# A softplus attention on one core: in each beat ScalarE takes the pending logarithm first and the exponentials second

## What is computed

```python
q, k, v = split(x @ w_qkv.T);  k_y = x @ w_ky.T          # 16 heads of 16
L   = einsum('bhqd,bhkd->bhqk', q, k) / 4
L_y = einsum('bhqd,bhkd->bhqk', q, k_y) / 4
agg = sum(exp(clip(L_y, -15, 15)) * causal, -1) + EPS
r   = log(abs(L) + EPS) - log(agg + EPS)
w   = softplus(r) * causal
A   = w / (sum(w, -1) + EPS)
x   = layernorm(x + (A @ v) @ w_proj.T)
x   = layernorm(x + ffn(x))                              # 256 -> 1024 -> 1024 -> 1024 -> 256
```

## Time and profile before

| | |
|---|---|
| device time, median of 3 runs | 1398.88 us (1397.62 to 1398.89) |
| the profiled execution: its own time | 1398.2 us |
| its span, first to last instruction | 1396.4 us |
| PE busy in the span | 1280.9 us (92%) |
| PE weight loads | 817.6 us (59%) |
| DVE busy | 718.2 us (51%) |
| ACT busy | 614.8 us (44%) |
| POOL busy | 113.3 us (8%) |
| mean granted TensorE clock | 0.972 |

### The profile page before, as it was taken

The page is one execution under the profiler, slowest core; times in us unless marked ns, Lnnn a source line. Parts: engine busy times, 40 slices in busy tenths (PEclk is TensorE's granted clock), DMA queues, the critical chain, the costliest instruction groups (busy, mean ns, idle before and its releaser), DMA issues.

```text
span 1396.4 us, 22945 instructions
## 1 busy us (share of the span) xinstructions
PE 1280.9 (92%) x8310; PEld 817.6 (59%) x8310; DVE 718.2 (51%) x1223; ACT 614.8 (44%) x810; POOL 113.3 (8%) x140
## 2 busy tenths in 40 slices
PE   5888999999898989977399999999999999999996
PEld 1433444434343434433278778787787878878785
DVE  2456777677676776566243532535326353353523
ACT  3566666666666666655042322323223241232411
POOL 1111121111111121110000000000000000000000
PEclk8999999999999999998589999999999999999998
DMA  2002222132122221000290000000000000000000
GB/s 74 16 16 69 92 75 77 60 102 78 60 90 90 90 71 57 1 31 31 70 331 15 16 15 15 30 15 19 11 15 30 15 30 0 15 30 15 30 0 16
DMA packets 31943, 66.89 MB, mean 48 GB/s; under 512 B 2848, under 2 KB 8608, under 8 KB 31904
## 3 DMA queue, kind: packets, MB, share of 16 engines
q1 hardware_dynamic: 31904, 66.35, 14.3%
HBM read 46.42 MB, written 19.92 MB: 48 GB/s over the span
## 4 chain that ended last, share of the span: by engine, by line
issue 50%; POOL 0%; DVE 0%; POOLq 0%; DVEq 0%
POOL f_rstd L809 0%; DVE f_res L816 0%; POOLq L909 0%; DVEq L821 0%; POOL f_minus_half L907 0%; POOLq L83 0%
## 5 line engine op out<-in xcount | busy, mean ns | idle before, releaser
L935 ACT ACTIVATE f_h_full<-f_layer_bank,f_scales 128x512 f32<-128x512 f32 x128 | 88.0, 687 | 354.8 <-PE f_layer_bank L1049 354.7
L500 DVE TENSOR_TENSOR w_ring<-score_banks,keep 128x1024 int32<-128x1024 int32 (+1 forms) x192 | 191.6, 1040 | 46.9 <-PE score_banks L649 46.9
L353 ACT ACTIVATE e_ring<-score_banks 128x1024 f32<-128x1024 f32 (+1 forms) x192 | 158.8, 879 | 122.8 <-PE score_banks L649 122.0
L1049 PE MATMUL f_layer_bank<-f_ha_hi,f_w_all 128*128 128x512 f32 x512 | 204.7, 400 | 2.7 <-DVE f_h_full L977 2.3
L1049 PE MATMUL f_layer_bank<-f_hb_hi,f_w_all 128*128 128x512 f32 x512 | 202.8, 396 | 0.0
L1049 PE MATMUL f_layer_bank<-f_ha_lo,f_w_all 128*128 128x512 f32 x512 | 202.1, 395 | 0.0
L1049 PE MATMUL f_layer_bank<-f_hb_lo,f_w_all 128*128 128x512 f32 x512 | 202.0, 395 | 0.0
L491 DVE TENSOR_SCALAR e_ring<-e_ring 128x2048 f32<-128x2048 f32 (+1 forms) x96 | 100.5, 1046 | 122.3 <-ACT e_ring L353 122.3
L360 ACT ACTIVATE w_ring<-w_ring 128x2048 f32<-128x2048 f32 (+1 forms) x96 | 156.8, 1633 | 8.6 <-DVE w_ring L500 8.3
L287 POOL TENSOR_SCALAR_AFFINE_SELECT e_ring<-e_ring 128x512 f32<-128x512 f32 (+1 forms) x96 | 78.5, 818 | 516.5 <-DVE e_ring L491 516.5
L675 PE MATMUL acc_bank<-w_ring,v_aug 128*32 128x512 f32 (+3 forms) x1024 | 91.2, 452 | 27.8 <-ACT w_ring L360 27.8
(11 more groups left out here) (101 smaller groups left out, 1535.0 us busy)
## 6 DMA issues: line engine op xcount, KB each, us to landing
piece<-in_wf SPq DMA_DIRECT2D x44, 256.0 KB, 2.9
wf_copy<-piece SPq DMA_DIRECT2D x44, 256.0 KB, 3.0
f_w_all<-wf_copy SPq DMA_DIRECT2D x2, 4096.0 KB, 26.4
f_x_turn<-x SPq DMA_DIRECT2D x9, 512.0 KB, 3.2
xq<-in_xt SPq DMA_DIRECT2D x8, 512.0 KB, 3.3
xv<-in_xt SPq DMA_DIRECT2D x8, 512.0 KB, 3.3
res<-in_xn SPq DMA_DIRECT2D x8, 512.0 KB, 4.6
x<-res SPq DMA_DIRECT2D x8, 512.0 KB, 2.6
```

What stands on the lines that cost most here:

```text
L353: nc.scalar.activation(e_ring[:, t % RING, 2 * i:2 * i + 2, 0:cols], pair_banks(y_pair(t, i), cols), ACT.Exp).then_inc(exp_done, 1)
L500: nc.vector.tensor_tensor(w_ring[:, t % RING, 2 * i:2 * i + 2, 0:cols].bitcast(I32), pair_banks(w_pair(t, i), cols).bitcast(I32), keep[:, ...
L935: nc.scalar.activation(h_full[m % 2][:], f_bank[m % RING][:], ACT.Gelu, scale=scales[:, 1 + layer, m:m + 1]).then_inc(gelu_done, 1)
L1049: mm = nc.tensor.matmul(out, left.bitcast(dt), right.bitcast(dt), start=first and n == 0, stop=last and n == 1)
```

## The change

ScalarE's slot issues the logarithm of the beat before ahead of this beat's exponentials, where it used to issue it behind them and behind one or two copies. Nothing is added or taken away, no wait is changed, and no other engine's order is.

```diff
             def slot(k, y=True, project=True, w=ALL, before=(True, True), out=None, check=None, **_):
                 for t in range(BEATS):
                     sums = sums_of(t, y, w, before)
+                    if sums[1]:
+                        logs(*beat_before(k, t))
                     if y:
                         exps(k, t)
                     if t == 0 and 3 in w:
                         v_sum_keep(k.shift(-1))
...
                     if t == 5 and y:
                         v_keep(k)
-                    if sums[1]:
-                        logs(*beat_before(k, t))
                     if t in (0, 1) and out is not None:
                         turn_keep(out, t)
```

## The result

The changed kernel takes 1439.81 us (median of 4 runs, 1436.95 to 1442.85), the kernel before 1398.25 (4 runs, 1394.01 to 1398.89). The ratio is 1.0304, with a 95% interval of 1.0274 to 1.0334: slower by 41.6 us. The prediction was 1445, with a range from 1422 to 1463. The profiled execution took 1439.41 us, with a span of 1437.7.

The account below looks back on a forecast made before the run. TensorE was the fullest engine, 92% busy; the new order closes a ring through ScalarE and VectorE. Slots 2 to 14 +41.9, slot 15 +2.4, slot 1 +1.4: 1398.2 + 45.7 = 1443.9; with 0.7 and 1 us, 1445; range 1422 to 1463.

Parts of the forecast that it names:

- The exponentials of beats 1, 2 and 4 are held up: ScalarE: exponentials go 1.7, 1.6 and at least 0.7 us later; small logarithms in beats 0 and 3 fit the gap.
- The ring of 7.31 us: ScalarE and VectorE: logarithm, exponentials, clip, absolute values, next logarithm in series; 7.31 us in beats 1 and 4.
- Beat 2, 7.14: Even slot: `scores_w(2)` comes 3.57 us behind `scores_y(2)`, with TensorE's queue full from there; 7.14 us, 5.80 before.
- Beat 4, 8.27: Even slot: logarithm waits behind the copy of the sums, +1.15, and query projection behind `keep_att`, +0.37; 6.75 becomes 8.27 us.
- Beat 5, 7.43: Even slot: 7.20 us plus 0.23 because the values' projection waits for VectorE's late part of `q_keep`.
- The sum, +45.7: Whole kernel: added time of slots 1 to 15; slot 0, slots after 15 and the feed-forward phase add 0.
- The 13 slots: Slots 2 to 14 of the attention phase, six with output projection: 550.5 us forecast against 508.6, +41.9.
- slot 15: Odd slot without TensorE projections for a next unit, more bound by the ring: 40.1 against some 37.7 us, +2.4.
- 1 us for the clock: Allowance kept because the granted clock fell to 0.50 in a few slots before, behind TensorE's waits of beats 1 and 2.
- the faster one: Rival: TensorE's 24.2 us of waits for the logarithm simply go, nothing else moves; 1374 us, chance 0.04.
- The half absorbed case: Rival: TensorE's backlog soaks up the ring, only the larger of ring and load counts per beat; +18, 1416, chance 0.18.
- The clock's rival: Rival: TensorE's waits lower its granted clock in each of 14 slots, +7 to +24; 1452 to 1469 us, chance 0.15.

Follow-up runs that it names:

- the pair of beats 0 and 3 alone: Logarithm ahead of the exponentials only in beats 0 and 3, old order elsewhere, against the kernel before: ratio 0.9991.
- the run with the copy in the ring: Changed kernel plus one 512-column ScalarE scratch copy in beat 1, between logarithm and exponentials: 1445.75 us, 1.0336 to the kernel before.
- the same copy outside it: Changed kernel plus the same scratch copy in beat 1, behind the exponentials and `keep_att`: 1438.82 us, 1.0289 to the kernel before.
- the narrow clip: Changed kernel with VectorE's clip on 128 columns a head only, the others left unclipped: 1420.34 us, 1.0151 to the kernel before.
- the cast's move: Changed kernel with ScalarE's cast in beat 3 (`piece_halve`) moved ahead of `ky_keep`: 1439.40 us, 1.0311 to the kernel before.
- the run with halves in beats 1 and 2: Kernel before with the logarithm cut in two in beats 1 and 2 only, first half ahead of the exponentials: 1389.37 us, 0.9945.

## Why the prediction was right, step by step

- *The exponentials of beats 1, 2 and 4 are held up, the small logarithms of 0 and 3 fit.* Right, and shown by the pair of beats 0 and 3 alone, at no cost.
- *The ring of 7.31 us sets beat 1.* Right: 7.29 in even and 7.30 in odd slots; the copy inside it cost its full 0.52, the same copy outside it nothing; a shorter clip shortened it, by 0.81 in odd slots and by 0.52 in even ones.
- *Beat 2, 7.14, by `scores_w(2)` late with TensorE full behind it.* Right: 7.13. In odd slots 5.41 said, 5.37 measured, and beat 3 there 6.13 and 6.15.
- *Beat 4, 8.27.* The mechanism held (the cast's move shortened it), the size was off: 8.01 and 8.10. The logarithm started 1.01 behind `scores_y(4)`, 1.02 said, though the copy ahead of it was not waiting for TensorE's sum, as I wrote, but stood behind the cast on ScalarE. The part that was too large is the 0.37 for the query projection behind `keep_att`. The timelines of ScalarE and TensorE:

```profile
359.37 0.42 ACT L402 COPY att_raw<-misc_bank 128x272 f32<-128x272 f32 x1
```
```profile
358.64 1.15 PE L649 MATMUL score_banks<-qc,key 32*128 32x128 f32 x16 [1.07 <-ACT e_ring L353]
359.84 1.98 PE L617 MATMUL misc_bank<-xq,w_in 128*128 128x512 f32 x4
```

  `scores_w(4)` stands 3.90 behind `scores_y(4)` (3.91 said); the projection starts 0.05 after the copy ends and 1.20 after `scores_w(4)`. Without a wait it would be the 1.08 of the kernel before, so the wait is worth 0.12.
- *Beat 5, 7.43.* 7.55, since that chain (`q_keep` on ScalarE, then on VectorE, then the values' projection) was a tenth later than I had it. VectorE's part in it is borne out by the narrow clip, with which beat 5 of even slots is 7.20.
- *The sum, +45.7.* Measured +41.6 by the medians. The 13 slots gave +39.8 where the sum had +41.9, and beat 4 is the largest part of the difference; slot 15 gave about +2.1 (said +2.4, though from 36.75 to 38.83 and not from 37.7 to 40.1), slot 1 +1.5 (said +1.4). These three make +43.4. The two profiled executions differ by 2.1 less, 1437.7 - 1396.4 = 41.3: the changed kernel's reached the copy of slot 1 at 47.02 us and the other's at 48.40, and behind the attention slots (from the copy of slot 16, at 666.34 and 624.30) the changed kernel's took 0.8 less. Neither comes from the new order, as far as the rows show. One slip in the sum itself: 1398.2 + 45.7 with the 0.7 and the 1 us is 1445.6, and I said 1445.
- *1 us for the clock.* The wrong way: the slots of the changed kernel show no fall at all, and the three odd slots of the kernel before with one add 1.7 us to the profiled time before.

So the mechanism was right, and 1445 is 5.2 us above the median of 1439.81. Of these, 2.3 are the sizes of the terms and 1 the allowance for the clock; the rest is of the size of what the two executions differ by at the start and the end, which no term of the sum foretold.

Of the rivals, the faster one fell with the list of waits: its 24.2 us did go, but the waits of TensorE for the exponentials ahead of its scores grew from 5.0 to 57.2 us. The half absorbed case (1416) would have had beat 2 at 5.8 and beat 4 at 7.3 in even slots. By the rule of the Trainium skill (Perfetto Trace Analysis, Optimization Strategy), to make start sooner what the most contended engine waits for, 1374 was to come; here the trace does not agree with it. The clock's rival did not occur: the granted clock was 1.00 in each stretch of 100 us from 100 to 600 us, with no wait on `scores_w` over 1.3 us. The Trainium skill (TensorE: Matmul & The Clock Gate, HAM oscillation) has it that waits between groups of matmuls can put the clock back; this run does not show it, the kernel before does in slots 5, 7 and 11, and the run with the copy in the ring in slots 4 to 7 and 9, below.

## What to carry to other kernels

Before one instruction is moved ahead of another on an in-order engine, compare when the inputs of both are ready, at each place of a repeating pattern: where the gap is larger than the moved instruction it is free (beats 0 and 3), where it is smaller the other is late by the difference. Then follow that one through the queues behind it; if they lead back to the input of the moved instruction, the durations around that ring are the new period wherever no engine's own work in the stretch is longer (beat 1 here, 7.29), whatever the busy shares say. Look also at what else stands ahead of the moved instruction in its own queue (the copy in beat 4). A cut of the instruction, so that its half with the early input goes first, kept the gain of the order without its price in beats 1 and 2, where the gap, counted from the half's own input, holds the half; in beats 4 and 5 it did not.

## What the runs showed of the hardware

- The granted clock of TensorE did not follow its busy share in a simple way. In the changed kernel, with waits of 1.07 to 1.26 us ahead of `scores_w` in three beats of each slot, and 500.27 us busy of the 587.0 between 76 and 663, it stayed at 1.00. In the kernel before TensorE was fuller, 433.95 us busy of the 469.44 from slot 4 on, and it fell in slots 5, 7 and 11, though not in 9 and 13. With 0.5 us more waiting in beat 1 (1.77 us ahead of `scores_w`), the run with the copy in the ring shows it low in slots 4 to 7 and 9, among them beat 1 of slot 4 and beat 2 of slot 5, in windows:

```profile
169.08:177.60 8.52, 6.70 (x57) 2.47 (x57) 6.30 (x11) 6.51 (x9) 1.10 (x1) 0.84 0.17 63
...
221.04:227.24 6.20, 6.20 (x53) 2.72 (x53) 4.52 (x8) 3.51 (x5) 0.76 (x2) 0.59 0.26 85
```

  Slot 5 there took 42.22 us against 41.51 in later odd slots, +0.71. The other four took no more than their like: in slot 4 beat 2 was shorter by the 0.7 that beat 1 was longer by (8.52 + 6.43 = 14.95, against 7.81 + 7.13 = 14.94 in slot 12). The three falls of the kernel before cost 0.53 to 0.62 each, those in the run with halves in beats 1 and 2 cost 1.18 to 1.30.
- Executions differ at the start. The copy in beat 0 of slot 1 comes behind work that is the same in all kernels but those that change the clip or VectorE's order, and it starts between 45.70 and 51.09 us in the profiled executions. The windows from 20 to 30 us of the earliest and the latest:

```profile
20.00:30.00 10.00, 8.10 (x67) 2.79 (x68) 3.15 (x3) 4.89 (x7) 2.45 (x3) 0.83 0.00 0
```
```profile
20.00:30.00 10.00, 6.59 (x48) 2.32 (x48) 3.15 (x3) 4.89 (x6) 2.25 (x3) 0.57 0.00 0
```

  The later one had the lower granted clock while TensorE had the same work ahead of it. That the clock is the whole cause is not shown: the kernel before had 0.52 in that window and started the copy at 48.40. The spread is 5.4 us between executions whose work up to there is the same, more than several of the effects above.
- An activation cut in two costs little here: 1.91 us whole (1.81 from start to start), 1.07 for each half and 0.96 from start to start, so about 0.1 us more in all.
